# Latent attention: copies and scalings moved from VectorE to ScalarE, latents turned one step later

## The reference, cut to what matters

```
q = (x @ Wq.T)                                  # 16 heads of 8
latent = layernorm(x @ Wdkv.T, ln_g, ln_b)      # 64 wide
k = latent @ Wuk.T ;  v = latent @ Wuv.T
q, k = apply_rope(q), apply_rope(k)
scores = where(causal, q.k / sqrt(8), -inf)
out = softmax(scores) @ v ;  return out @ Wo.T
```

## Time and profile before

| | us |
|---|---|
| median of 3 runs (2046.07 to 2053.31) | 2046.31 |
| the profiled execution | 2049.34 |
| its span | 2047.5 |
| latent attention, from its first negate of maxima to its last | 477.6 to 971.6 |
| TensorE, VectorE, ScalarE, GpSimd busy in the span | 1493.7, 1348.0, 1172.9, 773.1 |

### The profile page before, as it was taken

How to read it: one execution, slowest core, us unless ns; L and a number is a source line. 1 busy time by engine, 2 the same in 40 slices (tenths; PEclk the granted TensorE clock), 3 DMA queues, 4 the chain that set the end, 5 groups by cost and what they waited for, 6 DMA issues and landing times. The chain is left out here.

```text
span 2047.5 us, 63292 instructions
## 1 busy us (share of the span) xinstructions
PE 1493.7 (73%) x22193; PEld 1111.0 (54%) x22194; DVE 1348.0 (66%) x3733; ACT 1172.9 (57%) x2974; POOL 773.1 (38%) x823
## 2 busy tenths in 40 slices
PE   0688888846888877788424992888888884499991
PEld 0466666624555555556223780566666663377781
DVE  4577777636777777776454664678777875366665
ACT  2366666623544444444433990798888883377770
POOL 0000000022322323231485561336666666466661
PEclk9999999967999999999556995899999996699996
DMA  7110000000001000000012223000011111222227
GB/s 231 32 34 27 31 31 25 26 6 27 31 20 33 21 29 25 26 33 18 23 43 72 74 66 96 12 12 30 29 32 32 31 36 33 79 81 77 81 77 250
DMA packets 110889, 100.81 MB, mean 49 GB/s; under 512 B 17827, under 2 KB 98598, under 8 KB 110656
## 3 DMA queue, kind: packets, MB, share of 16 engines
q1 hardware_dynamic: 87648, 67.02, 11.0%
q0 software_dynamic: 12928, 25.60, 3.8%
q10 hardware_dynamic: 10080, 5.01, 0.8%
HBM read 43.25 MB, written 32.96 MB: 37 GB/s over the span
## 5 line engine op out<-in xcount | busy, mean ns | idle before, releaser
L2497 POOL DMA_INDIRECT e_back<-e_out_rows,e_G x142 | 148.4, 1045 | 98.8 <-issue 56.7
L664 DVE TENSOR_REDUCE m_mx<-m_pM 128x8 f32<-128x1024 f32 x128 | 155.6, 1216 | 29.6 <-PE m_pM L375 29.5
L1459 ACT ACTIVATE w_weights<-w_pS,w_ng 128x77 f32<-128x77 f32 x512 | 157.8, 339 | 17.7 <-DVE w_ng L1547 17.5
L526 ACT ACTIVATE m_PT<-m_pS 128x1024 f32<-128x1024 f32 x128 | 130.4, 1019 | 59.3 <-PE m_pS L404 58.0
L1112 POOL DMA_INDIRECT e_rows<-re_R,re_index x128 | 126.1, 985 | 63.7 <-issue 35.2
L526 ACT ACTIVATE a_PT<-a_pS 77x1024 f32<-77x1024 f32 x128 | 130.5, 1019 | 17.8 <-PE a_pS L404 12.6
L2520 DVE TENSOR_TENSOR e_gl<-e_g,e_gh 128x512 f16<-128x512 f32 x142 | 98.3, 692 | 57.4 <-ACT e_g L2464 53.7
L769 POOL TENSOR_SCALAR a_var<-a_aggr 128x4 f32<-128x4 f32 x16 | 3.1, 193 | 337.0 <-DVE a_aggr L590 337.0
L1660 POOL TENSOR_TENSOR w_weights<-w_weights,w_rec 128x616 f32<-128x616 f32 x64 | 77.9, 1217 | 125.4 <-DVE w_rec L1551 125.0
L664 DVE TENSOR_REDUCE a_mx<-a_pM 128x8 f32<-128x616 f32 x128 | 101.5, 793 | 33.0 <-PE a_pM L375 33.0
L1459 ACT ACTIVATION_READ_ACCUMULATOR w_weights<-w_pS,w_ng 128x1 f32 x512 | 113.6, 222 | 0.0
(11 more groups left out here) (383 smaller groups left out, 5651.1 us busy)
## 6 DMA issues: line engine op xcount, KB each, us to landing
e_G<-e_rows SPq DMA_DIRECT2D x106, 132.0 KB, 2.3
e_B<-e_back SPq DMA_DIRECT2D x16, 512.0 KB, 6.9
stage<-in_split SPq DMA_DIRECT2D x13, 512.0 KB, 4.6
Qs<-a_qh SPq DMA_DIRECT2D x128, 32.0 KB
Qs<-m_qh SPq DMA_DIRECT2D x128, 32.0 KB
Ks<-m_kh SPq DMA_DIRECT2D x32, 128.0 KB
e_R<-e_back SPq DMA_DIRECT2D x16, 256.0 KB, 3.5
w_stage<-in_late SPq DMA_DIRECT2D x16, 256.0 KB, 2.6
```

The source lines that it names most:

```text
L526: act.activation(PT[:NK, b % 2, 8 * half:8 * half + 8, :], pS[:NK, :, :], ACT.Exp, scale=float(1.0 / np.sqrt(HD))).then_inc(exp_done, 1)
L664: dve.tensor_reduce(out=mx[:, 8 * half:8 * half + 8], in_=pM[:, :, :NK], op=ALU.max, axis=AX.X).then_inc(m_max, 1)
L1459: ac = act.activation(weights[:, b % 2, n, :], pS[:, n // HB, n % HB, :KC], ACT.Exp, bias=ng[:, b % 2, n:n + 1], scale=float(WD) ** -0.5, ...
L2497: pool.indirect_dma_start(out=back, out_offset=bass.IndirectOffsetOnAxis(ap=G[:, r, s, D:D + 1].bitcast(I32), axis=0), in_=out_rows[:, r, ...
```

## The change

Five things are done, all in the latent attention.

- Four jobs go from VectorE to ScalarE: the copy of the maxima to `mT` (`keep_max`), the copies of the values (`v`), the scaling of the RMS norm (`rms_rows`), and the scale and shift of the turned latents, which ScalarE now does twice from PSUM, once to the high part `lh` and once to `lt` in full precision.
- The turned latents, `latT`, leave the last step of a group and are made in the first step of the next one, ahead of everything else there. They are now for the next group.
- The queries' product `q` moves from the start of step 0 to its middle, behind the first half of the maxima products; on VectorE its multiplication with `cos` stands behind the first reduction.
- On VectorE the scaling of the latents (`latents`) is separated from their statistics and stands behind the first reduction and the residual.
- On GpSimd the root of the RMS norm is taken ahead of the rotation of `ks`, and the low part of the latents stands in step 0, behind the root of the layer norm.

ScalarE's order within a step becomes: `keep_max`, then `latT` where there is one, `output_hi`, the first exponential, and then the rest as shown.

```diff
         if latent:
-            order = ["q", "qs", "k", "ks", "v", "x", "lat", "latT"]
-            first_use = 3
+            order = ["latT", "q", "qs", "k", "ks", "v", "x", "lat"]
+            first_use = 2
...
-            slots = {(0, 0): "q", (0, 1): "qs", (1, 0): "k", (1, 1): "ks", (2, 0): "v", (2, 1): "x",
-                     (3, 0): "lat", (3, 1): "latT"}
+            slots = {(0, 0): "latT", (0, 2): "q", (0, 1): "qs", (1, 0): "k", (1, 1): "ks", (2, 0): "v", (2, 1): "x",
+                     (3, 0): "lat"}
...
                 if more:
                     maxima(pn, bn, 0, gn)
+                what, gw, far = slot(b, 2, g, nxt, nxt2)
+                if what:
+                    project(what, gw, None)
                 if two:
                     turn_output(*two)
...
+                elif what == "v" and latent:
+                    act.wait_ge(used, u + 1)
+                    wait(act, pv_ready, lin(g, GB, -GB))
+                    settle(act, c)
+                    for b in range(GB):
+                        cp = act.activation(V[:NK, p, b, :, 0:HD],
+                                            pP[:NK, b * P:(b + 1) * P].rearrange("k (h d) -> k h d", h=H), ACT.Copy)
+                    cp.then_inc(evac, 1)
                 elif what == "latT":
-                    act.wait_ge(evac, u + 1)
-                    act.activation(lh[:], lt, ACT.Copy).then_inc(hi_made, 1)
+                    act.wait_ge(used, u + 1)
+                    wait(act, lat_lo, lin(g, 1, 0))
+                    settle(act, c)
+                    act.activation(lh[:], pP[:LAT, :TG], ACT.Identity, scale=SM("lg", LAT),
+                                   bias=SM("lb", LAT)).then_inc(hi_made, 1)
+                    act.activation(lt, pP[:LAT, :TG], ACT.Identity, scale=SM("lg", LAT),
+                                   bias=SM("lb", LAT)).then_inc(evac, 1)
...
+            def rms_rows(g):
+                act.wait_ge(ms_done, lin(g, 1, 1))
...
+                for b in range(GB):
+                    act.activation(xn[:, b:b + 1, :], Y[:, bass.ds(lin(g, GB, b), 1), :], ACT.Copy,
+                                   scale=rr[:, b:b + 1]).then_inc(rms_r, 1)
+
+            def keep_max(g, b):
+                act.wait_ge(mt_ready, lin(g, GB, b + 1))
+                wait(act, s_ready, lin(g, 2 * GB, 2 * (b - 1)))
+                act.activation(mT[:, b % 2, :], pTh[:], ACT.Copy).then_inc(mt_kept, 1)
...
+                if latent:
+                    keep_max(g, b)
+                if first and (first == "latT" or not latent):
+                    part(first, ga, (p + far_a) % 2)
                 if two:
                     output_hi(*two)
                 exps(g, p, b, 0)
+                if first and first != "latT" and latent:
+                    part(first, ga, (p + far_a) % 2)
                 if one:
                     keep_heads(*one)
                 if latent and b == 1 and nxt2:
                     squares(shift(g, 2))
...
+                if latent and b == 2 and nxt2:
+                    rms_rows(shift(g, 2))
+                late = second in ("qs", "ks")
+                if second and not late:
+                    part(second, gb, (p + far_b) % 2)
                 exps(g, p, b, 1)
                 if late:
-                    part(what, gw)
+                    part(second, gb, (p + far_b) % 2)
...
                 if more:
                     take_max(gn, bn, 0)
+                middle, gm, far = slot(b, 2, g, nxt, nxt2)
+                if middle:
+                    part(middle, gm, (p + far) % 2)
                 if two:
                     residual(*two)
...
-                if latent and b == 2 and nxt2:
-                    rms_rows(shift(g, 2))
+                if what == "lat":
+                    latents(gw)
                 if more:
                     take_max(gn, bn, 1)
                     negate(gn, bn)
...
-                for half_ in (0, 1):
+                for half_ in (0, 2, 1):
                     what, gw, far = slot(b, half_, g, nxt, nxt2)
+                    if b == 1 and half_ == 1 and nxt2:
+                        squares(shift(g, 2))
                     if what:
                         rope(what, gw)
-                if b == 1 and nxt2:
-                    squares(shift(g, 2))
```

More of the change, by code:

```diff
@@ L274, in slot @@
             what = slots.get((b, half))
-            if what in ("x", "lat", "latT"):
+            if what in ("x", "lat"):
                 return (what, shift(g, 2), 2) if nxt2 else (None, None, 0)
             return (what, shift(g, 1), 1) if what and nxt else (None, None, 0)
-        start_x = ["x", "lat", "latT"] if latent else ["x"]
-        start = ([(w, 0) for w in start_x] + [(w, 0) for w in order if w not in start_x]
-                 + [(w, 1) for w in start_x])
+        if latent:
+            start = [(w, 0) for w in ("x", "lat", "latT", "q", "qs", "k", "ks", "v")] + [("x", 1), ("lat", 1)]
+        else:
+            start = [("x", 0), ("q", 0), ("k", 0), ("v", 0), ("x", 1)]
         def earlier(g, b, by):
@@ L298, in hi_count @@
             per = [w for w in order if w in (("x", "qs", "ks", "latT") if latent else ("x", "q", "k"))]
-            lead = 2 if latent else 1
-            back = 1 if what in ("x", "latT") else 0
+            lead = 1
+            back = 1 if what == "x" else 0
             return lin(g, len(per), lead + per.index(what) + 1 - back * len(per))
@@ L489, in _, with part @@
         def _(act):
-            def part(what, g):
+            def part(what, g, p):
                 u = use(g, what)
@@ L546, in begin @@
                 for what, k in start:
-                    if latent and what == "x" and k == 1:
-                        squares((None, 1))
-                    part(what, (None, k))
+                    if latent and what == "x":
+                        if k == 1:
+                            squares((None, 1))
+                        rms_rows((None, k))
+                    part(what, (None, k), k)
             def step(g, p, b, nxt, nxt2):
                 one, two = earlier(g, b, 1), earlier(g, b, 2)
-                what, gw, far = slot(b, 0, g, nxt, nxt2)
-                if what:
-                    part(what, gw)
+                first, ga, far_a = slot(b, 0, g, nxt, nxt2)
+                second, gb, far_b = slot(b, 1, g, nxt, nxt2)
+                if latent:
+                    keep_max(g, b)
+                if first and (first == "latT" or not latent):
+                    part(first, ga, (p + far_a) % 2)
                 if two:
@@ L562, in step @@
                     squares(shift(g, 2))
-                what, gw, far = slot(b, 1, g, nxt, nxt2)
-                late = what in ("qs", "ks")
-                if what and not late:
-                    part(what, gw)
+                if latent and b == 2 and nxt2:
[3 more added lines that the diff above has]
+                    part(second, gb, (p + far_b) % 2)
                 exps(g, p, b, 1)
                 if late:
-                    part(what, gw)
+                    part(second, gb, (p + far_b) % 2)
             def finish():
@@ L633, in part @@
                                       ALU.mult).then_inc(evac, 1)
-                elif what == "v":
+                elif what == "v" and not latent:
                     dve.wait_ge(used, u + 1)
@@ L648, in part, with latents @@
                         dve.bn_aggr(laggr[:, b, :], lstats[:, b, :]).then_inc(lat_agg, 1)
-                    dve.wait_ge(lat_rstd, lin(g, 1, 1))
-                    for b in range(GB):
-                        ts = dve.tensor_scalar(latn[:, b, :], pP[:, b * LAT:(b + 1) * LAT], laggr[:, b, 0:1],
-                                               lrstd[:, b:b + 1], ALU.subtract, ALU.mult)
-                    ts.then_inc(evac, 1)
-                elif what == "latT":
-                    dve.wait_ge(used, u + 1)
-                    wait(dve, lat_lo, lin(g, 1, 0))
-                    dve.tensor_scalar(lt, pP[:LAT, :TG], SM("lg", LAT), SM("lb", LAT), ALU.mult,
-                                      ALU.add).then_inc(evac, 1)
+            def latents(g):
+                dve.wait_ge(lat_rstd, lin(g, 1, 1))
+                for b in range(GB):
+                    ts = dve.tensor_scalar(latn[:, b, :], pP[:, b * LAT:(b + 1) * LAT], laggr[:, b, 0:1],
+                                           lrstd[:, b:b + 1], ALU.subtract, ALU.mult)
+                ts.then_inc(evac, 1)
             def take_max(g, b, half):
@@ L713, in begin @@
                         norm_rows((None, k))
-                        if latent:
-                            rms_rows((None, k))
                     part(what, (None, k), k)
+                    if what == "lat":
+                        latents((None, k))
                 take_max((None, 0), 0, 0)
@@ L726, in step @@
                 two = earlier(g, b, 2)
-                keep_max(g, b)
+                if not latent:
+                    keep_max(g, b)
```

12 lines of the change are left out of this document (4 added, 8 removed).

## The result

The changed kernel takes 2068.49 us (median of 4 runs, 2065.3 to 2077.25), the kernel before on the same chip 2047.95 (4 runs, 2046.07 to 2053.31). The ratio is 1.0103, with an interval of 1.0064 to 1.0142: it is slower by some 20 us. The profiled execution is the longest of the four, 2077.25, and its span of 2075.4 is 28 above that of before.

The account below looks back on a forecast made before the run. No engine fills a group; an engine chain and a transfer chain end together. Nine groups with jumps +13.7, four groups +2.8, edges −0.7, low clock +2: +17.8 on 2049.34 gives 2067.1, as a median 2064; own range 2055 to 2072.

Parts of the forecast that it names:

- Step 0: Group's first step: first reduction 1.08 us later behind ScalarE's two latent writes, queries' multiplication adds 0.65; 6.91 to 8.64.
- Step 1: Second step: queries' sum waits for the latents' low part, +0.73, plus copy of the maxima, 0.16; 7.69 us.
- Step 2: Third step: RMS root ahead of the keys' sum delays the first reduction, VectorE saves work; 8.08 us, +0.53.
- Step 3: Last step: ScalarE's queue delays the key-dependent matmul to 3.0, the tail loses the 1.52 stall; 8.07 us, −0.82.
- The transfers: SyncE's chain from queries' low part to keys: 26.09 us against a matmul due at 27.4, so 1.3 early.
- VectorE's relief: Rival, chance 0.14: ScalarE's insertions hide in idle time, group 28.7 us, 1.5 shorter in 13 groups; 2026.
- A clean group: Undisturbed latent attention group, four steps summed: 32.48 us, +2.33 over the clean 30.15.
- The jump: Groups after the loop's jump, where TensorE starts late: 2.8 us each, four jumps counted.
- low clock: Spells of low granted clock in the latent groups: +2 us in all, from 0 to +12.
- The first group: First latent group has no output to turn: −0.6 us.
- the last but one of the groups: Its queries are late too: +0.9 us.
- The last group: Its copy of the maxima has a free engine: 0 change.

Follow-up runs that it names:

- split alone: Kernel before, with only the latents' scaling on VectorE moved behind the first reduction and the residual: 2028.76 us, ratio 0.9903.
- the other moves: Changed kernel with all four jobs back on VectorE, the new places and GpSimd's new order kept: ratio 0.9983 against the kernel before.
- the shift: Kernel before with all four jobs on ScalarE, old slots, GpSimd's old order and the latents' scaling in its old place: 2053.85 us, ratio 1.0018.
- the undoings: Changed kernel with one PSUM read of the latents, their low part first, RMS root after the keys, maxima copied on VectorE: 2026.82 us, ratio 0.9893.
- two edits to the split: Kernel before, latents' scaling behind the first reduction, value copies and RMS scaling on ScalarE, key transfers on ScalarE's queue; both together 2054.59 us, ratio 1.0042.

## Why the prediction came out as it did

The forecast was 2064, slower by the chain of engines, and that is what happened; the measured 2068.5 lies in its own range. By its steps:

- **Step 0, forecast 8.64, measured 8.43.** Right in its mechanism: the product's start (2.65 forecast, 2.66 measured), its wait for the second read (1.09), the first reduction (4.29 and 4.14). Taking that second read away gave back the 0.66 that it put on the path. `lh` and `lt` took 0.773 and 0.762 (medians of 16) where I took 0.777 from the earlier trace rows. The Trainium skill, "ScalarE: Activation LUTs", section What ACT_TABLE_LOAD costs, states what an activation takes by its columns and what each pointer operand adds; an estimate from its figures is 799 ns, and the trace has 26 to 37 ns less. The output was turned 3.32 after the negate (3.40), and the reduction began 0.82 after that instead of 0.88.
- **Step 1, 7.69 and 7.51.** The root ended 0.34 after the negate and the low part followed at once; it ran until 1.45, so the queries' sum came at 1.41 rather than 1.60. With the low part first 0.53 of it went, and with the copy of the maxima on VectorE 0.16.
- **Step 2, 8.08 and 8.06.** The keys' sum came at 2.16 (2.2), the first reduction at 4.66 (4.69). Moving the root back gave 1.30 in this step.
- **Step 3, 8.07 and 7.84.** The key-dependent matmul came at 2.83 (3.0), its tail was 5.01 (5.04), and the stall of 1.52 went. The split alone shows that stall as worth all of its 1.52.
- **The transfers** were to be early, and were: no wait on them in a clean group after.
- **VectorE's relief** doesn't count, which was the rival on the other side. The Trainium skill, "Perfetto Trace Analysis", section Optimizing Scalar/DVE Operations, says that it may make sense to offload some work to Scalar if DVE is saturated. Here VectorE was busy for 80% of a group without being what the group waited for, and moving the four jobs alone cost 0.65 us: the one gain was 0.77 in step 2, and ScalarE's longer queue took 1.27 in step 3.

Four terms of the sum were off. A clean group is 31.84 and not 32.48, which over the 13 groups 1 to 13 made my sum 8 us too large. The jump was too small: I had +2.8 a time, and the four steps behind a jump were 12.93, 11.71, 12.37 and 12.43, +3.9 over a clean 8.44. TensorE's own stall there is unchanged (2.89, 2.83); the rest came at a mean granted clock of 0.72 to 0.85 in these steps, where three of the four such steps before had 1.00 and one 0.84. I had +2 for low clock altogether; groups 5, 9 and 13 (33.90, 32.79, 33.86) add 5 to the clean length, and groups 1 to 4 one more. The first group came out 1.0 longer, where I had −0.6, and the last but one of the groups, for which I had +0.9, 0.45 shorter. The last group's 15.66 is unchanged, as forecast. So the two main errors, 8 too much on clean groups and some 9 too little on jumps and clock, about cancel. The mechanism of the clean steps was right; that the total came within 5 us was in part luck.

What the change did, on a clean group: 30.15, less 1.52 for the stall, plus 1.36 for the other moves (29.99 − 28.63), plus 1.85 for the shift on top of them (31.84 − 29.99). The first figure was measured alone; the other two are differences of kernels. The moves' 1.36 I haven't split further without the shift. After the undoings, the one step that stays longer than in the split alone is step 0 (7.77, and 7.70 with the latents on VectorE, against 6.91), with the latents and the queries' product in one step; steps 2 and 3 together are as long as there (14.94 and 14.92).

What stays open is why the low clock falls where it does. In the seven kernels with `latT` in step 0, all 28 such steps behind a jump had a mean granted clock of 0.72 to 0.86, and were 3.3 to 4.5 us longer than the clean step 0. In the kernel before and the five others without it there, 11 of 24 had 1.00 and the rest 0.70 to 0.84, and they were 2.3 to 5.3 longer. So low clock behind a jump goes with the new step 0, though it occurs without it. No experiment made a gap longer or shorter for this alone.

## What to carry to other kernels

When no engine fills the span, read what each in-order queue holds ahead of the instruction that the next engine waits for, and move that instruction; here one operation moved behind a reduction was worth 1% and three transfers on another queue another 1%, while taking all four jobs off VectorE, 3.1 us of its work in every group, made the clean group longer. Each added instruction is to be placed where its engine stands idle anyway: the same three issues of transfers gained 1% in one kernel and cost 35 us in the next. Test the parts one by one, and then the pairs that you mean to keep, since they didn't add up in either pairing tried here (moves and shift cost 1.36 and 0.65 us a group apart, 3.2 together; and two edits to the split, neither of which had made it slower, made it slower than the kernel before).

## What the runs showed of the hardware

- Issuing a transfer isn't free for the engine that does it. On SyncE one of the keys' mostly took 0.58 to 0.60 us and one of the queries' 0.67; on ScalarE the three of the keys took 1.8 to 2.6 us together, at the longest shown 0.54, 1.32 and 0.62, with 2.32 us in which its next activation didn't start.
- An activation with scale and bias both from memory took 0.76 to 0.77 us for 64x512 from PSUM, some 0.08 more than one of 128x512 with the scale alone and some 0.17 more than one with neither.
- The same 252 matmuls at the end of the first attention took 14.4 us in one execution and 20.8 in another, at a granted clock of 1.00 and 0.50, though nothing ahead of them differs in the code. That one spell is worth 6.4 us of a single execution, so a difference of that size is to be read from medians.
